# Attention steps one half pair later, second transposed chunk in another bank, strips of scores alternating

## The reference

```python
q, k, v = (xn @ W.T + b for each of the three)         # 16 heads of 16
scores = where(mask, (q @ k.T) * SCALE, -10000.0)      # mask: j <= i and j >= i - 128
attn = softmax(scores) + 1e-9
attention = (attn @ v) @ Wo.T + bo
h = silu(xn @ shared_gate) * (xn @ shared_up)          # and the same in the chosen experts
ffn = h @ shared_down + sum over the 2 experts of p_e * expert_e(xn)
out = x + attention + ffn
```

## Time and profile before

| what | us |
|---|---|
| median of 3 runs | 2126.1 |
| the runs | 2117.62 to 2126.46 |
| the profiled execution | 2116.85 |
| its span in the trace | 2115.1 |
| one turn of the last stage (the one at 1554.82) | 55.09 |

### The profile page before, as it was taken

How to read it: one execution, slowest core, us unless ns; L and a number is a source line. 1 busy time by engine, 2 the same in 40 slices (tenths; PEclk the granted TensorE clock), 3 DMA queues, 4 the chain that set the end, 5 groups by cost and what they waited for, 6 DMA issues and landing times.

```text
span 2115.1 us, 40817 instructions
## 1 busy us (share of the span) xinstructions
PE 1737.2 (82%) x12377; PEld 1482.9 (70%) x12378; DVE 1251.5 (59%) x3737; ACT 882.7 (42%) x1721; POOL 774.1 (37%) x725
## 2 busy tenths in 40 slices
PE   6936455544999999999999888888888888888887
PEld 6925454443888888888888667666666677666666
DVE  6653232322666666666666657766766667776762
ACT  2211111112454545555555345544554554555552
POOL 0014423320000000000000057777777777777775
PEclk9998777676999999999999869999999998999998
DMA  8347767665444444444444456767777777777752
GB/s 281 131 148 231 221 211 225 213 211 187 149 152 150 152 150 150 150 148 154 149 151 150 103 139 161 166 154 166 165 165 161 164 171 166 166 165 165 165 144 81
DMA packets 262429, 350.61 MB, mean 166 GB/s; under 512 B 26736, under 2 KB 172400, under 8 KB 260336
## 3 DMA queue, kind: packets, MB, share of 16 engines
q1 hardware_dynamic: 210304, 278.21, 47.4%
q0 software_dynamic: 12288, 33.57, 6.2%
q10 hardware_dynamic: 39792, 38.28, 5.5%
HBM read 219.43 MB, written 129.50 MB: 165 GB/s over the span
## 4 chain that ended last, share of the span: by engine, by line
PE 57%; issue 12%; SPq 11%; DVE 9%; DMA 6%; ACT 4%; POOL 1%; DVEq 0%; ACTq 0%; POOLq 0%
PE psum L149 31%; PE psum L784 10%; SPq L577 9%; PE psum L1263 6%; PE psum L1227 4%; DVE plain_arena L1430 4%; DMA plain_arena<-xn_d 3%; PE psum L1249 2%; PE psum L855 2%; DVE split_arena L1440 1%; ACT plain_arena L1357 1%; PE psum L1276 1%; DVE plain_arena L1449 1%; ACT plain_arena L1363 1%; SPq L580 1%
## 5 line engine op out<-in xcount | busy, mean ns | idle before, releaser
L149 PE MATMUL psum<-split_arena 128*128 128x256 f32 (+1 forms) x5328 | 994.1, 343 | 32.2 <-DVE plain_arena L1453 13.8
L149 PEld LDWEIGHTS psum<-split_arena 128*128 128x128 f32 x5328 | 840.7, 200 | 146.5 <-DVE plain_arena L1453 24.3
L1430 DVE CUSTOM_DVE_ANT_0 plain_arena<-psum,mask 128x256 f32<-128x256 f32 (+1 forms) x1024 | 337.5, 384 | 235.1 <-PE psum L1227 218.7
L1357 ACT ACTIVATE plain_arena<-psum 128x512 f32<-128x512 f32 (+1 forms) x512 | 252.3, 546 | 409.1 <-PE psum L1249 388.1
L1212 POOL MEMSET split_arena<- 128x256 f32 x1 | 0.3, 311 | 699.0 <-ACTq L138 699.0
L784 PE MATMUL psum<-split_arena 128*128 128x256 f32 x1872 | 233.8, 285 | 0.0
L784 PEld LDWEIGHTS psum<-split_arena 128*128 128x128 f32 x1872 | 226.9, 192 | 0.1
L1227 PE MATMUL psum<-split_arena 48*128 48x256 f32 (+1 forms) x1024 | 177.2, 359 | 35.8 <-DVE plain_arena L1430 24.8
L614 POOL DMA_INDIRECT sorted_d<-plain_arena,q_idx x128 | 124.1, 970 | 199.5 <-DVE q_idx L701 163.8
L1159 POOL TENSOR_SCALAR_AFFINE_SELECT plain_arena<-plain_arena 128x1024 f32<-128x1024 f32 x128 | 140.0, 1094 | 148.6 <-ACT plain_arena L1357 146.4
L901 ACT ACTIVATE plain_arena<-psum 128x512 f32<-128x512 f32 x156 | 93.3, 598 | 220.0 <-PE psum L149 219.8
(11 more groups left out here) (132 smaller groups left out, 2030.0 us busy)
## 6 DMA issues: line engine op xcount, KB each, us to landing
plain_arena<-in_gate_w SPq DMA_DIRECT2D x39, 512.0 KB, 5.0
plain_arena<-in_up_w SPq DMA_DIRECT2D x39, 512.0 KB, 6.1
plain_arena<-in_down_w SPq DMA_DIRECT2D x39, 512.0 KB, 6.9
plain_arena<-sorted_d SPq DMA_DIRECT2D x39, 512.0 KB, 3.8
y_d<-plain_arena ACTq DMA_DIRECT2D x39, 512.0 KB, 3.6
plain_arena<-in_x SPq DMA_DIRECT2D x32, 512.0 KB, 3.9
plain_arena<-xn_d SPq DMA_DIRECT2D x32, 512.0 KB
q_d<-split_arena SPq DMA_DIRECT2D x64, 256.0 KB
```

Source lines behind the costliest of these rows:

```text
L149: last = pe.matmul(out, lhs_t(p), rhs(q), start=(begins and c == 0 and k == 0), stop=(ends and c == len(chunks) - 1 and k == 2), skip_grou ...
L1357: act.activation(b_pt[:, g % 2, 2 * p + par, 4 * half:4 * half + n, :].rearrange("p k s -> p (k s)"), psum[:, 2 + par, 0:n * P], ACT.Exp, ...
L1430: last = dve.tensor_tensor_reduce(b_junk[:, 2 * par + i % 2, 0:cols], psum[:, par, at:at + cols], mask[:, 2 * P - cols:2 * P], -1.0, 3e38, ...
```

## The change

It has four parts.

1. Every lag of the attention behind the maxima grows by one half pair; `load_v` moves with them. The masked maxima, the products of the shared expert and the two kinds of projection stay where they are.
2. The rows are transposed at h = 3 and 4 and no longer at 5 and 6. The second chunk goes to bank 4, the bank of the values' sums. It waits for the copy of the second group's sums, and the third group's values wait for both chunks to be read.
3. In `scores` and `scores_t` the two strips alternate (one matmul of each head, then the other of each), and there is one wait for both heads' banks together in place of one for each.
4. The loads of queries and keys move: groups 1, 2 and 3 of the sequence come at h = 0, 4 and 8 and group 0 of the next at h = 12. Before, groups 2 and 3 came at 3 and 7, groups 0 and 1 of the next sequence at 11 and 15.

```diff
-        LAG_TM, LAG_M, LAG_T, LAG_SEL, LAG_V, LAG_U = 4, 5, 7, 9, 13, 14
-        LAG_US, LAG_UL, LAG_RC, LAG_SP, LAG_N, LAG_CH, LAG_CL = 15, 16, 18, 19, 21, 22, 23
+        LAG_TM, LAG_M, LAG_T, LAG_SEL, LAG_V, LAG_U = 5, 6, 8, 10, 14, 15
+        LAG_US, LAG_UL, LAG_RC, LAG_SP, LAG_N, LAG_CH, LAG_CL = 16, 17, 19, 20, 22, 23, 24
...
-                    b, g = due_group(t, h, 6)
+                    b, g = due_group(t, h, 7)
                     if b is not None:
                         load_v(b, g)
-                    if h in (3, 7) and valid(t):
-                        load_qk(sp, t, 2 + h // 7)
-                    if h in (11, 15) and valid(t + 1):
-                        load_qk(sp, t + 1, h // 15)
+                    if h in (0, 4, 8) and valid(t) and not (h == 0 and is_first(t)):
+                        load_qk(sp, t, 1 + h // 4)
+                    if h == 12 and valid(t + 1):
+                        load_qk(sp, t + 1, 0)
...
-                for par in range(2):
-                    rows = slice(64 * par, 64 * par + 48)
-                    after(pe, b_mx, 32 * b + 2 * r + par - 1)
-                    for i in (2 * half, 2 * half + 1):
+                after(pe, b_mx, 32 * b + 2 * r)
+                for i in (2 * half, 2 * half + 1):
+                    for par in range(2):
+                        rows = slice(64 * par, 64 * par + 48)
...
-                    last.then_inc(b_s, 1)
+                        if i % 2 == 1:
+                            last.then_inc(b_s, 1)
...
-                if g == 1:
-                    after(pe, b_xlo, 2 * b)
+                if g == 0:
+                    after(pe, b_xlo, 2 * b - 1)
...
                 after(pe, b_ue, 4 * b + g)
+                if g == 2:
+                    pe.wait_ge(b_xlo, 2 * b + 2)
...
                 if c == 0:
                     pe.wait_ge(b_ldx, 16 * b + 16)
-                    pe.wait_ge(b_nc, 4 * (b + 1) + (1 if valid(b + 1) else 0))
+                    pe.wait_ge(b_nc, 4 * b + 4)
                 else:
-                    pe.wait_ge(b_xlo, 2 * b + 1)
+                    pe.wait_ge(b_ue, 4 * b + 2)
                 for a in range(T):
-                    last = pe.transpose(psum[:, 5, a * P:(a + 1) * P],
+                    last = pe.transpose(psum[:, 5 - c, a * P:(a + 1) * P],
...
-                    if h in (5, 6) and valid(t - 1):
-                        turn_rows(t - 1, h - 5)
+                    if h in (3, 4) and valid(t - 1):
+                        turn_rows(t - 1, h - 3)
```

More of the change, by code:

```diff
@@ L1243, in scores_t @@
                     pe.wait_ge(b_ldm[g % 2], 32 * (2 * b + g // 2) + 32)
-                for par in range(2):
-                    rows = slice(64 * par, 64 * par + 50)
-                    after(pe, b_ex, 32 * b + 2 * r + par - 1)
-                    for j in (2 * half, 2 * half + 1):
+                after(pe, b_ex, 32 * b + 2 * r)
+                for j in (2 * half, 2 * half + 1):
+                    for par in range(2):
+                        rows = slice(64 * par, 64 * par + 50)
                         cols = P if j == T - 1 else 2 * P
@@ L1252, in scores_t @@
                                          start=True, stop=True)
-                    last.then_inc(b_t, 1)
+                        if j % 2 == 1:
+                            last.then_inc(b_t, 1)
             def values(b, g):
@@ L1405, in turn @@
                         hidden_hi(b, m)
-                    if h in (6, 7) and valid(t - 1):
-                        rows_hi(t - 1, h - 6)
+                    if h in (4, 5) and valid(t - 1):
+                        rows_hi(t - 1, h - 4)
                     b, c = due_chunk(t, h, LAG_CH)
@@ L1500, in turn @@
                         reciprocals(b, c)
-                    if h in (6, 7) and valid(t - 1):
-                        rows_lo(t - 1, h - 6)
+                    if h in (4, 5) and valid(t - 1):
+                        rows_lo(t - 1, h - 4)
                     b, c = due_chunk(t, h, LAG_CL)
```

4 lines of the change are left out of this document (2 added, 2 removed).

## The result

The changed kernel takes 2150.6 us (median of 4 runs, 2135.38 to 2165.69) where the kernel before takes 2122.9 (4 runs, 2117.62 to 2126.46): 1.0135 times the time, 95% interval 1.0088 to 1.0181. It is slower. The prediction was 2077 us, with 0.08 on slower. Its profiled execution took 2165.55 us, so the trace is of one of the two longer runs; the other two took 2135.4 and 2135.6.

What follows compares the result with a forecast made beforehand. The prediction saw a turn bound by a chain passing between engines, its idle time between h = 15 and h = 9. 2116.85 - 46 (turns) + 8 (joint wait) - 5 (end) = 2074 us, given as 2077; forecast 2060 to 2100, 8-in-10 range 2035 to 2112.

Steps and rivals of the forecast that it cites:

- the second part: Rest of a turn, from PE's scores of h = 9 to DVE's maxima of h = 15: 20.71 us, no gain expected.
- the joint wait: One wait for both heads' banks in the scores: +7 us in turn 0, +1 at the start of turn 1.
- ACT, DVE or late loads take the place of the stall: Rival: the gain is eaten, about 1.2 us a turn is left, 2103 us; chance 0.2.
- The first part: From DVE's maxima of h = 15 to PE's scores of h = 9: 34.38 us, forecast 3.3 shorter.
- the stall of 43.0 us: PE's second chunk of transposed rows waits for DVE's `rows_lo` 16 times; 2.7 us a turn, forecast to go.
- the walk: Step-by-step timing from the maxima of h = 15 to the scores of h = 9: 4.0 us saved, 3.3 taken.
- The lower clock at h = 2: PE's values there run at the lower clock, 2.88 us, after PE stood; projection between 1.42 and twice that.
- the sign: What would show the forecast: DVE's idle time before the maxima of h = 2 under 1 us.
- The loads: Moved query and key loads land 1 us before the scores of h = 4, the same at h = 12; charged 0.
- the bad end: Worst case for the moved loads and reciprocals: 1 us a turn, +14 us.
- The strips: Alternating the strips in the scores' matmuls, costed at nothing because they already run side by side when queued.
- The end: Kernel's end: 24 matmuls remain behind the context, net -3.5 us; with turn 16's own stall saved, -5 together.

Runs made afterwards that it cites:

- the third experiment: The changed kernel without part 3 (heads one after the other, a wait for each): 2121.1 us, ratio 1.0022 to the kernel before.
- the sixth experiment: The changed kernel with `context_lo` ahead of the maxima and DVE's reciprocals one half pair earlier: 2107.5 us, ratio 0.9946 to the kernel before.
- the two repairs: `context_lo` ahead of the maxima and reciprocals one half pair earlier, put into the changed kernel; with part 3 also taken out: 2092.7 us, ratio 0.9868.
- the fifth experiment: The kernel before with part 3 alone (strips alternating, one wait for both heads' banks): 2126.3 us, ratio 1.0029 to the kernel before.

## Why the prediction was wrong

- **The step that failed** is the sentence on the second part: "I see no gain: PE's work is the same, what ACT has to do only trades places". It spoke of PE, ACT and the joint wait, and never of what DVE's `context_lo` does at h = 12. Its lag of 24 put it beside GpSimd's mask, bias and `hidden_lo`. The second part was 21.42 us in the shortest turn (20.71 forecast), 22.7 on the mean of the nine turns without the hold, and 29.68 in a held one. The hold is shown from both sides: moving the call alone took 41 us from the changed kernel, and moving the lag alone made the kernel before slower by 2.2%. No rival held this mechanism either; "ACT, DVE or late loads take the place of the stall" had DVE's busy time in mind, and priced the whole at a loss of the gain, not at a loss below it.
- **The first part** was right in mechanism and nearly in size. Forecast 31.1, measured 31.42 in the turn shown and 31.9 on the mean of the nine; the stall of 43.0 us gone, the matmuls behind it at 1.43. But the later lags have no share in it: the two banks alone, with the lags of before, bring this part to 30.0. They brought 36 us, and the walk had 46 for the turns.
- **The lower clock at h = 2** was foreseen and a little short (3.10 for 2.88, the projection 1.62 within its bounds). DVE's idle time before those maxima was 1.03, where under 1 was the sign. That the later lags with the moved loads cost some 9 us net, against the two banks alone with the old lags, was not seen: I had counted them as a gain.
- **The joint wait**: +8, of it +7 in turn 0. Measured 41.2 for 33.3 in turn 0, and 6 us alone. Right as a term; in the changed kernel more turns are held with it than without it (24 us by the ratios between the third experiment and the changed kernel, turn 0 included), and that part was not in the sum.
- **The loads**: "1 us to spare ... I charge 0". As a wait it was wrong: 2.0 us on the mean of 17 places, twice the bad end, and at h = 12, where the walk only says that "the same holds". At h = 4, which it reckoned, the keys came in time. In the turns without the hold this wait is most of the 2.2 us that the second part loses. What it costs in time is not shown: its removal brought nothing measurable in the sixth experiment, beside a call already moved. I reckoned 10.6 us from the end of the reciprocals to the last landing, and it is 13.7 (1615.80 to 1629.53). Most of the difference is the last transfer, 6.07 us where I took 4.3.
- **The strips** at nothing: right. Part 3 alone left the mean turn at 54.68 for 54.88, and in the chain four matmuls of scores take 0.43 us (1602.05) for 0.44.
- **The end**: -5 forecast. From the last scores to the end of the kernel it is 63.6 us for 66.7, so -3. The picture behind it was wrong: 72 matmuls still follow the last `hidden_lo` (L1172), and not 24, since that one comes behind other work of GpSimd's. The chain's end:

```profile
2146.90 1.27 POOL split_arena L1172
...
2148.22 11.43 PE psum L149 x72
```

**The sum again**, by differences of the ratios, times 2122.9: the two banks -37 (0.9825), the later lags and the moved loads, with the two repairs, +9 (to 0.9868), part 3 beside them +17 (to 0.9946), the later reciprocals 0 (to 0.9948), the hold +40 (to 1.0135; of four runs that lie in two pairs 30 us apart). That it closes at +29 is by construction; the prices are those of this order of mending, and the fifth experiment shows that part 3 costs only 6 in another.

## What to carry to other kernels

When a change moves an operation of DVE by a step, lay it beside what GpSimd does in that step, also when its own cost and its readers say that it has room: a row "busy" much longer than its shortest form is a wait that the list of waits doesn't hold. Price each edit of a bundle where it can be seen alone; here one of four brought all of the gain, and a lag that was moved only to keep company took it back and more. And a wait that ends last on an engine is worth its length only if nothing else would have ended just after it: taking away 33 us of late loads brought nothing that could be measured, and taking away 27 us of PE's waits for the split in the kernel before brought a new wait of the same size.

## What the runs showed of the hardware

Some of DVE's operations, when they start while GpSimd runs operations with no gap between them, are not let in between two of them. `context_lo` lasted until 0.55 us after the run was over: 7.1 to 7.5 us over the rest of a run of seven in the changed kernel, 8.4 us in every turn with the loads first, 6.2 over five in the kernel before with the later lag. With waits of GpSimd for its own operations in the run the longest was 2.4, and a gap of 0.18 us let it in. Other operations of DVE are not held at all. In the changed kernel's last stage those that read psum keep their time beside GpSimd's runs (maxima 0.43 us at most, products 0.43, `rows_lo` 0.69), and so do the reciprocals, which read and write SBUF (0.54). The held ones are `context_lo`, both operations of the split and, for up to 1.2 us, some small copies (128 x 8 and 128 x 2 elements).

The Trainium skill, "SBUF — State Buffer", section "Who interferes with whom", says that a DVE instruction with two SBUF inputs contends with a GpSimd instruction that reads SBUF, and that whoever issues first has the shared pair of ports for the whole instruction. The kinds agree: `context_lo` has two inputs in SBUF, and all seven neighbours read there. The duration does not: by that rule one instruction of at most 1.3 us would have been waited for, and the row shows the rest of seven. Why the ports don't pass over in the seam between two of them stays open; the runs show only that a gap lets DVE in.

The hold isn't a matter of size. The split's first operation, 128 x 16 elements and one input, takes 0.174 us when free and was held for up to 3.1 us in the kernel with the two banks alone.
